# Seven first steps of the window-attention layers put inside the last batch's tail of the ball block

## What is computed

```python
x = x + attn(cond(x, c))               # mixture of experts, then memory attention: block "moe_attention"
x = x + ffn_layers(cond2(x, c))        # cond2: the "ball" block; ffn_layers: two window-attention layers

def cond2(x, t_emb):                   # hyperbolic transformer block, 8 batches of 512 rows
    ada = t_emb @ w_ada + b_ada                                  # scale, shift and gate, twice
    xm = expmap0(layer_norm(logmap0(x)) * (1 + sc_msa) + sh_msa)
    attn = softmax(q k^T / 4) v;  x = mobius_add(x, expmap0(g_msa * logmap0(attn_out)))
    xm = expmap0(layer_norm(logmap0(x)) * (1 + sc_mlp) + sh_mlp)
    return mobius_add(x, expmap0(g_mlp * logmap0(plin(plin(xm, w_f1), w_f2))))

def layer(x):                          # twice, over all 8 batches
    q, k, v = split(shift_token(x) @ wqkv)                       # 8 heads of 64
    q, k = rotary_xpos(l2norm(q) * qs, l2norm(k) * ksc)
    x = x + local_attention(q, k, v) @ wo                        # window of 128 rows, look one window back
    h = layer_norm(shift_token(x)) @ w1 + b1;  a, g = split(h)
    return x + (a * gelu(g)) @ w2 + b2
```

## Time and profile before

| | us |
|---|---|
| median of 3 runs (lowest, highest) | 3371.13 (3369.37, 3375.45) |
| the profiled execution's own time | 3368.89 |
| its span, first to last instruction | 3367.1 |
| ball block's first load issued | 1142.4 |
| last ball batch: last matmuls of the attention | 1847.9 to 1849.0 |
| ball block's last store issued | 1969.5 |
| window layers' first instruction | 1973.0 |

### The profile page before, as it was taken

How to read it: one execution, slowest core, us unless ns; L and a number is a source line. 1 busy time by engine, 2 the same in 40 slices (tenths; PEclk the granted TensorE clock), 3 DMA queues, 4 the chain that set the end, 5 groups by cost and what they waited for, 6 DMA issues and landing times. The chain is left out here.

```text
span 3367.1 us, 53624 instructions
## 1 busy us (share of the span) xinstructions
PE 3142.3 (93%) x18984; PEld 1774.3 (53%) x18984; DVE 2103.0 (62%) x6476; ACT 1706.6 (51%) x3219; POOL 560.1 (17%) x696
## 2 busy tenths in 40 slices
PE   7999999999996788998998758999999999999998
PEld 3455555555554433444344435566666666666665
DVE  3233343343346567778776648777777777777783
ACT  2243343433443366656555325666666666666662
POOL 0000000000002334434442221111111111111110
PEclk9999999999998799999999889999999999999999
DMA  5110111101100200000000030000000000001000
GB/s 191 58 54 29 56 38 48 67 32 42 60 10 14 87 9 9 7 17 15 12 13 13 10 146 23 17 23 23 23 23 26 23 23 29 29 29 29 24 25 29
DMA packets 77763, 120.81 MB, mean 36 GB/s; under 512 B 10083, under 2 KB 66088, under 8 KB 72376
## 3 DMA queue, kind: packets, MB, share of 16 engines
q1 hardware_dynamic: 77496, 117.37, 10.3%
HBM read 96.33 MB, written 16.83 MB: 34 GB/s over the span
## 5 line engine op out<-in xcount | busy, mean ns | idle before, releaser
L2608 PE MATMUL wps<-w_wqkv,w_hT 128*128 128x512 f32 x768 | 375.8, 613 | 3.1 <-DMA w_wo<-in_wwo 3.1
L1244 ACT ACTIVATE bb_pr<-ps 128x2048 f32<-128x2048 f32 x128 | 240.2, 1877 | 245.3 <-PE ps L1763 244.7
L2201 POOL TENSOR_TENSOR w_rn<-w_n,w_mhalf 128x16 f32<-128x16 f32 x64 | 186.4, 2913 | 1006.5 <-DVE w_n L2395 1006.5
L1179 POOL TENSOR_TENSOR b_routs<-b_rins,b_expo 128x4 f32<-128x4 f32 x88 | 89.9, 1022 | 1387.3 <-DVE b_rins L1398 1387.3
L2646 PE MATMUL wps<-w_xnT,w_w 128*128 128x512 f32 (+1 forms) x704 | 317.3, 593 | 2.6 <-DVE w_xnT L2458 1.4
L2229 ACT ACTIVATE w_pr<-w_sm,w_nmx,w_rn 128x256 f32<-128x256 f32 (+1 forms) x512 | 286.9, 566 | 1.1 <-DVE w_nmx L2376 0.3
L635 PE MATMUL ps<-xT,b_late 128*128 128x512 f32 x512 | 247.6, 606 | 4.3 <-DMA rb<-in_eb 4.3
L651 PE MATMUL ps<-hid,b_late 128*128 128x512 f32 x512 | 240.8, 592 | 0.0
L2646 PEld LDWEIGHTS wps<-w_xnT,w_w 128*128 128x128 f32 (+1 forms) x704 | 132.2, 188 | 151.6 <-issue 146.4
L2608 PEld LDWEIGHTS wps<-w_wqkv,w_hT 128*128 128x128 f32 x768 | 132.0, 191 | 121.0 <-issue 121.0
L2238 ACT ACTIVATE w_qkr<-wps 128x512 f32<-128x512 f32 x128 | 75.5, 590 | 233.7 <-PE wps L2608 233.7
(11 more groups left out here) (330 smaller groups left out, 6430.0 us busy)
## 6 DMA issues: line engine op xcount, KB each, us to landing
b_late<-in_ew SPq DMA_DIRECT2D x32, 1024.0 KB, 6.8
w_xa<-xs SPq DMA_DIRECT2D x16, 512.0 KB, 3.9
w_xin<-xs SPq DMA_DIRECT2D x64, 128.0 KB, 4.2
xT<-in_xT SPq DMA_DIRECT2D x8, 512.0 KB, 3.8
xres<-in_x SPq DMA_DIRECT2D x32, 128.0 KB, 2.2
x<-x1t SPq DMA_DIRECT2D x32, 128.0 KB, 1.7
b_mod<-ada SPq DMA_DIRECT2D x16, 256.0 KB, 3.1
xs<-bb_wb SPq DMA_DIRECT2D x8, 512.0 KB, 2.9
```

Source lines behind the costliest of these rows:

```text
L1244: a.activation(pr[:, G % 2], ps[:, SC:SC + 4], ACT.Exp, scale=DH ** -0.5).then_inc(p_ok, 1)
L2201: g.tensor_tensor(rn[:, i % 2, t], n2[:, n % 2, 1], mhalf[:], ALU.pow).then_inc(nr_ok, 1)
L2608: ins = te.matmul(to, hT[:, i % 2, k, t * P:(t + 1) * P], wqkv[:, i // B, k, s * 512:(s + 1) * 512], start=(k == 0), stop=(k == KD - 1))
```

## The change

The last block becomes two pieces. `layer_parts` holds its step functions, and `ball_block` calls them for steps -8 to -2 at its own steps of the table; `layer_block` runs the rest from step -1. For that, buffers of the layers that these steps need must exist while the ball block runs: a common memory `Shared` (26,624 words a partition) holds them on top of ball buffers that are dead by then (`wqkv`, `hT` over `late`; `rots`, `qT` over the probabilities; `qkr`, `qk`, `kT`, `rot` over the odd batches' q, k, v; `vt`, `xin`, `yt` over the rows `xb`). The same memory holds weights and buffers of `moe_attention`. `ident` and the PSUM tensor are common to all blocks, so `ident` is loaded once.

```diff
+AHEAD_OF_LAYERS = {131: -8, 132: -7, 133: -6, 135: -5, 137: -4, 159: -3, 163: -2}
...
+        WEIGHTS, TABLES = parts.S * (B - 1) + 1, parts.S * B + 1        # 113, 129
         @block.sync
         def _(sp):
             step = parts.sync_steps(sp)
+            ahead = layers.sync_steps(sp)
             for G in STEPS:
                 step(G)
+                if G == WEIGHTS:
+                    sp.wait_ge(parts.pv_mm, parts.S * (B - 1))
+                    sp.wait_ge(parts.out_ok, 3)
+                    sp.wait_ge(parts.st_x, 3 * 16)
+                    layers.first_loads(sp)
+                if G == TABLES:
+                    sp.wait_ge(parts.pv_mm, parts.S * B)
+                    layers.table_loads(sp)
+                if G in AHEAD_OF_LAYERS:
+                    ahead(AHEAD_OF_LAYERS[G])
...
+    def first_loads(sp):
+        sp.dma_start(xa, xs[0].rearrange("(t p) d -> p t d", p=P)).then_inc(ld_xa, 16)
+        sp.dma_start(wqkv[:, 0], io["wqkv"][0]).then_inc(ld_q[0], 16)
+    def table_loads(sp):
+        sp.dma_start(rot, io["rot"]).then_inc(ld_c, 16)
+        sp.dma_start(qks.rearrange("p l a b v -> p l (a b v)"), io["qks"]...).then_inc(ld_c, 16)
+    def loads(sp):                       # at the head of layer_block
+        sp.dma_start(wmask[:], io["wmask"]).then_inc(ld_s, 16)
+        for l in range(NL):
+            if l:
+                sp.dma_start(wqkv[:, l], io["wqkv"][l]).then_inc(ld_q[l], 16)
+            sp.dma_start(wo[:, l], io["wwo"][l]).then_inc(ld_f[l], 16)
...
+    def tables(dve):                     # DVE, behind ball step 129
+        v.memset(hT[:, :, 1, 0:1], 0.0).then_inc(pre_ok, 1)
+        dve.wait_ge(ld_c, 2 * 16)
...
+    def constants(dve):                  # DVE, head of layer_block
+        v.memset(hs[:, :, 0], 0.0).then_inc(pre_ok, 1)
+        v.memset(st[:], 0.0).then_inc(pre_ok, 1)
+        v.memset(h2T[:, MH - 1], 1.0).then_inc(pre_ok, 1)
+        v.memset(ps[:, 0:2], 0.0).then_inc(pre_ok, 1)
+        dve.wait_ge(pre_ok, PRE)
+        dve.wait_ge(ld_s, 16)
...
+        def project_heads(i, t):
+            if t == 0:
+                pe.wait_ge(ld_f[i // B], NLOAD_F * 16)      # wo now counts with the feed-forward weights: 5 loads
...
+def layer_block(nc, layers):
+        STEPS = range(max(AHEAD_OF_LAYERS.values()) + 1, layers.STEPS[-1] + 1)     # from -1
```

More of the change, by code:

```diff
@@ L862, with ball_parts @@
     pass
[L865 removed]
+def ball_parts(nc, io, x1, xs, outer, shared):
     NH, DH = 16, 16
@@ L1917, in _ @@
             step = parts.vector_steps(dve)
+            ahead = layers.vector_steps(dve)
             for G in STEPS:
                 step(G)
+                if G == TABLES:
+                    layers.tables(dve)
+                if G in AHEAD_OF_LAYERS:
+                    ahead(AHEAD_OF_LAYERS[G])
         @block.tensor
@@ L1923, in _, with layer_parts @@
             step = parts.tensor_steps(pe)
+            ahead = layers.tensor_steps(pe)
             for G in STEPS:
                 step(G)
-def window_layers(nc, io, xs, x1, out):
+                if G == TABLES:
+                    pe.wait_ge(layers.pre_ok, layers.PRE_AHEAD)
+                if G in AHEAD_OF_LAYERS:
+                    ahead(AHEAD_OF_LAYERS[G])
+def layer_parts(nc, io, xs, x1, out, whole, shared):
     NL = 2
@@ new lines, in layer_parts, with attends, phase @@
+    pT_mm, pT_a, pT_v, pv_mm, oT_ok = sem("pT_mm"), sem("pT_a"), sem("pT_v"), sem("pv_mm"), sem("oT_ok")
+    ve_in, ve_ok, xn_ok = sem("ve_in"), sem("ve_ok"), sem("xn_ok")
+    mixed_gelu = sem("mixed_gelu")
+    v_t = sem("v_t")
+    chained, turn = [0], [0]
+    NLOAD_F = 5
+    STEPS = range(-U, U * NI + 2 * U + NT)
+    def attends(G):
+        return 0 <= G < U * NI
+    def phase(G, start, period, count):
+        for n in range(count):
+            i, rest = divmod(G - start - period * n, U)
+            if rest == 0 and 0 <= i < NI:
+                return i, n
+        return None
@@ new lines, in layer_parts, with bank, filled, emptied @@
+    place = {}
+    for G in STEPS:
+        for job in side_jobs(G):
+            place[job] = (5 + len(place) % 3, len(place) // 3)
+    def bank(*job):
+        return ps[:, place[job][0]]
+    def filled(eng, *job):
+        k, n = place[job]
+        eng.wait_ge(full[k], n + 1)
+    def emptied(eng, *job):
+        k, n = place[job]
+        eng.wait_ge(free[k], n + 1)
+    def heads(half):
+        return [(g, c2, 2 * half + c2) for g in range(2) for c2 in range(2)]
+    def first_loads(sp):
+        sp.dma_start(xa, xs[0].rearrange("(t p) d -> p t d", p=P)).then_inc(ld_xa, 16)
+        sp.dma_start(wqkv[:, 0], io["wqkv"][0]).then_inc(ld_q[0], 16)
@@ L2102, in side_jobs @@
[L2102 to L2124 removed]
+                input_turned(turn_x(G)[0])
@@ L2701, in _chunks @@
+            pe.wait_ge(layers.pre_ok, layers.PRE)
+            step = layers.tensor_steps(pe)
+            for G in STEPS:
+                step(G)
 def _chunks(w):
```

1292 lines of the change are left out of this document (653 added, 639 removed).

## The result

The changed kernel takes **3349.09 us** (median of 4 runs, 3346.93 to 3351.89); the kernel before took 3370.64 in the runs beside it. The ratio is 0.9936, interval 0.9921 to 0.9951: 21.6 us less. Forecast were 3350.3 us, 0.994, and the range 3341 to 3361. The profiled execution after took 3346.93 us with a span of 3345.1, its fastest run; before it was 3367.1.

What follows compares the result with a forecast made beforehand. PE was taken to bound the layers, no engine the whole tail, DVE a stretch inside it. Gain 35.0 less tail cost 14.2 (7.5 + 3.4 + 3.3) gave 20.8 us saved: 3350.3 us, range 3341 to 3361.

Steps and rivals of the forecast that it cites:

- Front: Last block's start to attention step 0's first exponential (the mark): 9.3 us instead of 44.3, gaining 35.0 us.
- Step 129: Ball block: DVE's memset and eight table instructions, 3.4 us at most, fit its 3.50 us idle; costs nothing.
- Step 131: Ball block: DVE's copy of the turned input stands ahead of batch 7's `update`, costing 1.7 us.
- Additions of POOL: Tail: POOL additions beside DVE's work; taken as zero, with 2 us either way for each of two moved pairs.
- No slack gives it back before the feed-forward of batch 7: Tail: the 7.5 us that early insertions add to DVE's chain stay until batch 7's feed-forward.
- Step 159: Ball block: DVE does `keys` and `row_norms` before returning to the third tile's rows, costing 3.4 us.
- Step 163: Ball block: DVE's `rotate` stands between asking for the root and reading it, costing 3.3 us.
- Behind the mark all engines run the same list: After attention step 0's first exponential, engines do the same work in both kernels; no loss was counted.
- (a): Rival: the tail's waits absorb the insertions, which cost 5 to 10 us; 3341 to 3345 us, at 3343; 18%.
- (b): Rival: tail insertions dear through passed-on waits and half clock, 6 to 10 us more; 3356 to 3360 us; 17%.
- (c): Rival: the last block's start does not gain, something such as late weights sets the first exponential; 3366 us; 4%.
- (d): Rival: new buffer places slow each of 128 attention steps, with 0.3 us a step giving 3388 us; 3%.

Runs made afterwards that it cites:

- loads_only: Changed kernel with no step moved; early loads, tables and common memory stay, last block starts with step -8: 3362.36 us, ratio 0.9975 to the kernel before.
- power_later: Changed kernel with POOL's power of step -5 queued behind the additions of ball step 136 instead of ahead of them: 3348.55 us.
- five_only: Changed kernel with the last two insertions, steps -3 and -2, put back at the head of the last block: 3349.82 us, ratio 0.9940.
- keep_clock: Changed kernel with 18 unused PE transposes before each of item 1's four waits for rotated heads: 3342.54 us, ratio 0.9919.
- before_keep: Kernel before with 18 unused PE transposes before each of item 1's four waits for rotated heads, nothing of the change: 3369.59 us, ratio 0.9987.

## Why the prediction was right, and where not

The time was right to 1.2 us, by the mechanism that was forecast. In the profiles the 22.0 us are: 36.2 gained at the front, 11.7 paid in the tail, 2.9 lost behind the mark, and 0.4 gained ahead of the ball block, which is scatter. Forecast were 35.0, 14.2, nothing and nothing. So the errors cancel to 1.2 us in the spans: 1.2 more gained, 2.5 less paid, 2.9 lost, 0.4 of scatter. That the time came so close is luck; the mechanism of the front and of the tail was right, term by term below. The median's 1.2 us is within the scatter of the runs as well.

- *Front*, 9.3 forecast, 8.15 measured. The v columns came at half clock as taken, but in 2.96 us, not 3.4. With the same list it took 2.96 to 3.73 us in six kernels. The other 0.7 us is ACT, which began `queries` 0.2 us behind the first transpose and not 1.0.
- *Step 113*: nothing. *Step 129*: cover of 3.50 us, 0.92 left; right. With the early loads and the tables alone, in `loads_only`, the ball block was 0.8 us longer. In that profile `result` of batch 6 took 3.69 us, as in the changed kernel, and 2.68 before, which is more than the whole difference.
- *Step 131*: 1.7 forecast, 1.35 measured.
- *Projections at 133 to 137*: nothing, right; PE waited 11.37 us for DVE ahead of batch 6's second product.
- *Row norms*: 1.4 and 1.33.
- *Additions of POOL*: zero taken, with 2 us either way for each pair. Here the sum was mis-sized. The first pair gave back 2.03 us at `result` and took 0.6 elsewhere. The second pair cost the rotation 1.95 and gave back 1.87 in `row_angles`. The net is 1.35 of the 2.0 us between 7.5 and 5.5, and most of the rest is step 131. The shared interface's rule holds for the rotation in the trace (its second instruction took 2.17 us here and 1.23 in the rotation at step 163), yet it would have been wrong to charge it alone. The Trainium skill, SBUF — State Buffer, section SBUF: two separate sides, says more: the shared pair is locked for the whole of an instruction, and the other engine waits. In steps of about one addition's time (1.22 to 2.17, 0.17 to 1.26, the addition pair 2.67 to 3.84) the trace agrees. It does not agree for the power: 3.08 us on POOL, and the four `result` instructions beside it took 1.67.
- *"No slack gives it back before the feed-forward of batch 7"*: 5.5 us at batch 6's second product and 5.4 at batch 7's, but by luck. Between them 1.7 us of clock were gained and 1.6 lost, of which the forecast had none. With batch 6's last second product as slow as in `power_later`, the tail would have been near 13.4 us dearer (an estimate, 11.7 + 1.7) and the profile 1.7 us longer.
- *Step 159*: 3.4 and 3.06. *Step 163*: 3.3 and 3.15. `five_only` gives 6.4 for both.
- *"Behind the mark all engines run the same list"*: true, but it does not follow that they take the same time. This is the step that failed, by 2.9 us. Stands of PE that were there before are followed by half clock or not. `keep_clock` with `before_keep` shows that this is the difference: with the stands partly filled, mark to end is 1347.19 and 1347.13.

Of the rivals, (a), cheap insertions, came true in part: `result` was relieved by 2 us, as it said. Its time, 3341 to 3345, did not (35.0 less 10 below 3371.1 makes 3346 at the upper end, not 3345). (b) did not, with no wait at 133. Its half-clock mechanism was there in part where it was put (6.64 us, for 6.09 before and the 7.1 it feared), and cost more behind the mark. (c) fell: the first projection through `wo` ran at 2019.14 with no wait of PE just ahead of it, and the DMA share had dropped from 0.84 to 0.10 by 2007. (d) fell: from the sixth projection on the steps have the length of before, so the common memory costs nothing there.

Of the signs named, the last store (11.6 us late, in the window of 11 to 18), the mark (8.15, in the window of 8 to 12) and the length of the steps came true; "21 us earlier from there" was 24.9 and then 22.0. Others missed. The block started 11.3 us later and not 14, and the first exponential came at 1992.5, not 1997. The last second product of batch 7 was 8.0 us late, where 10 to 11 were forecast (the early 5.4 in place of 7.5, and 2.6 for the two jobs ahead of it).

**Open.** Why the clock fell at the first stand in the changed kernel and only later in the kernel before, behind the same 3.54 us, was not found. Nor was it why PE ran at 5.30 us in one kernel and 3.62 in the other at batch 6's last second product. Mark to end lies between 1349.7 and 1352.6 in the seven profiles without the extra transposes, and there is one profile of each. So neither the 2.9 us lost nor the 1.7 us gained has been shown to be a property of the change. That the additions can be kept away from DVE's chain altogether was not tried.

## What to carry to other kernels

When work is moved into another stage's gaps, each engine's share has its own gap: one table for all engines cost 11.7 us of tail; a table of DVE's own, with one step moved for all, cost 4.2, and 7.2 in another profile. Follow the neighbours on GpSimd as well as the moved instruction; a collision that it takes over is relieved somewhere else, and only the difference counts. And look at the granted clock behind each stand of TensorE: unused transposes in four such stands here were worth 5.4 us behind the mark, and made the part behind it repeat to 0.1 us. Where a forecast agrees with a time to 1 us, add up its terms against the trace before you believe it: here gains and losses of 1 to 3 us hid each other.

## What the runs showed that was not expected

- Mark to end is 1347.13, 1347.15, 1347.15 and 1347.19 us in the four kernels with the extra transposes, and 1349.73 to 1352.62 in the others.
- The same stand of 3.54 us was followed by the full clock in one kernel and by half in the other. In the tail, a stand of 3.71 us and eight transposes were followed by a second product of 3.62 us in three profiles, of 5.30 or 5.31 in four, and of 4.72 to 5.10 in the other four.
- The first block, in which all kernels have the same instructions, ended between 1140.66 and 1146.59 us.
- A VectorE instruction of 128 x 4 elements with one tensor operand took 1.26 us beside GpSimd's additions, 0.17 otherwise; a reduction of 128 x 1024 beside them kept its 1.21.
- Unused work on a TensorE that has stood still is not free: 16 transposes behind a stand of 11.82 us took 3.65 us and delayed the scores by 1.4.
